# A factorization-machine kernel on one core: the raw quad moved to sixth place with a signal of its own, and VectorE scaling two quads of a block

## The reference

```python
gathered = jax.vmap(lambda table, idx: table[idx], in_axes=(0, 1), out_axes=1)(emb, xi)
e = gathered * xv[:, :, None]
s = jnp.sum(e, axis=1)
qi = 0.5 * (s * s - jnp.sum(e * e, axis=1))
h = jax.nn.relu(xv @ W1 + b1)              # hidden: 1024
x = jnp.concatenate([qi, h], axis=1)
return x @ W2 + b2                         # one number per sample
```

## Time and profile before

| | us |
|---|---|
| median of 3 runs (lowest to highest) | 735.56 (734.74 to 735.95) |
| the profiled execution | 734.71 |
| its span, first to last instruction | 732.9 |
| DVE busy | 540.5 |
| POOL busy | 485.9 |
| ACT busy | 474.2 |
| PE busy | 123.1 |

### The profile page before, as it was taken

How to read it: one execution, slowest core, us unless ns; L and a number is a source line. 1 busy time by engine, 2 the same in 40 slices (tenths; PEclk the granted TensorE clock), 3 DMA queues, 4 the chain that set the end, 5 groups by cost and what they waited for, 6 DMA issues and landing times.

```text
span 732.9 us, 2598 instructions
## 1 busy us (share of the span) xinstructions
PE 123.1 (17%) x374; PEld 29.6 (4%) x374; DVE 540.5 (74%) x463; ACT 474.2 (65%) x516; POOL 485.9 (66%) x524
## 2 busy tenths in 40 slices
PE   2030020300303003030211302203030220400315
PEld 0000000000000000000000000001000000000001
DVE  4675969595398683988969396396978849549684
ACT  0877775771875837778683863868777394567871
POOL 6777775762767737777774754777777474677760
PEclk9995555555555555555555555555555555555557
DMA  7777775772766737777774763777777474577760
GB/s 226 203 204 203 204 203 158 203 204 56 202 192 185 205 102 204 203 204 204 203 202 128 202 179 98 203 203 204 203 204 202 126 203 132 145 203 203 203 190 0
DMA packets 33683, 131.93 MB, mean 180 GB/s; under 512 B 8641, under 2 KB 8769, under 8 KB 33634
## 3 DMA queue, kind: packets, MB, share of 16 engines
q0 software_dynamic: 32768, 130.06, 64.6%
q1 hardware_dynamic: 800, 1.31, 0.6%
q10 hardware_dynamic: 98, 0.40, 0.2%
HBM read 131.72 MB, written 0.01 MB: 180 GB/s over the span
## 4 chain that ended last, share of the span: by engine, by line
POOL 39%; issue 23%; another core or an unknown queue 6%; PE 3%; DVE 2%; ACT 1%; DMA 0%; POOLq 0%
POOL gathered L218 39%; DVE running_ps L462 1%; PE sum_ps L328 1%; PE hidden_ps L349 1%; ACT squares L241 1%; ACT squares L247 1%; PE hidden_ps L362 1%; PE sum_ps L341 1%; DMA gathered<-emb,index_rows 0%; DVE squares L435 0%; DVE gathered L447 0%; POOLq L214 0%; DVE weighted_late L547 0%; DVE weighted L421 0%
## 5 line engine op out<-in xcount | busy, mean ns | idle before, releaser
L218 POOL DMA_INDIRECT gathered<-emb,index_rows x512 | 484.4, 946 | 224.1 <-issue 155.8
L462 DVE SCALAR_TENSOR_TENSOR running_ps<-gathered,running_ps 128x1984 f32<-128x1984 f32 x77 | 171.4, 2226 | 146.7 <-issue 107.6
L435 DVE SCALAR_TENSOR_TENSOR squares<-squares,w_ps 128x1984 f32<-128x1984 f32 (+1 forms) x128 | 276.7, 2167 | 0.0
L234 ACT ACTIVATE gathered<-gathered,values 128x496 f32<-128x496 f32 x312 | 194.5, 695 | 25.5 <-DMA gathered<-emb,index_rows 23.3
L241 ACT ACTIVATE squares<-gathered 128x5952 f32<-128x5952 f32 x31 | 159.8, 5156 | 36.8 <-DMA gathered<-emb,index_rows 34.3
L341 PE MATMUL sum_ps<-added_up,own_sample 128*32 128x496 f32 x128 | 30.1, 1031 | 550.3 <-issue 431.0
L247 ACT ACTIVATE squares<-gathered,values 128x496 f32<-128x496 f32 x76 | 47.4, 696 | 67.4 <-DMA gathered<-emb,index_rows 63.2
L362 PE MATMUL hidden_ps<-w_b,value_rows 33*128 33x512 f32 x64 | 55.3, 1011 | 42.4 <-issue 20.8
L234 ACT ACTIVATE running_ps<-gathered,values 128x496 f32<-128x496 f32 x64 | 39.5, 662 | 33.7 <-issue 18.7
L254 ACT ACTIVATE sum_squared<-sum_ps 128x496 f32<-128x496 f32 x16 | 9.2, 573 | 71.0 <-remote 58.4
L462 DVE SCALAR_TENSOR_TENSOR added_up<-gathered,running_ps 128x1984 f32<-128x1984 f32 x16 | 35.5, 2219 | 25.4 <-ACT gathered L234 25.0
(11 more groups left out here) (40 smaller groups left out, 27.0 us busy)
## 6 DMA issues: line engine op xcount, KB each, us to landing
gathered<-emb,index_rows POOLq DMA_INDIRECT x512
w_all<-w SPq DMA_DIRECT2D x1, 760.0 KB
values<-value SPq DMA_DIRECT2D x1, 256.0 KB, 2.9
value_rows<-value_t ACTq DMA_DIRECT2D x1, 256.0 KB
index_raw<-index SPq DMA_DIRECT2D x1, 240.0 KB, 4.3
w_b<-w ACTq DMA_DIRECT2D x1, 128.0 KB
index_raw<-index SPq DMA_DIRECT2D x1, 16.0 KB, 2.5
w_b<-b ACTq DMA_DIRECT2D x1, 4.0 KB
```

The costliest lines, as they stand in the source:

```text
L218: nc.gpsimd.indirect_dma_start(out=gathered[:, n % slots, j, :], out_offset=None, in_=emb, in_offset=bass.IndirectOffsetOnAxis(ap=index_ro ...
L234: return nc.scalar.mul(running_ps[:, j, 0:dim] if s == 0 else rows_of_one, rows_of_one, values[:, g:g + 1])
L435: return nc.vector.scalar_tensor_tensor(of, of, -0.5, w2_ps[:, 0:dim].unsqueeze(1).to_broadcast([P, quads_of.stop - quads_of.start, dim]), ...
L462: nc.vector.scalar_tensor_tensor(added_up[:, i % 2] if last_add(n) else sums, gathered[:, n % slots], 1.0, sums, ALU.mult, ALU.add).then_i ...
```

## The change

The raw quad of a block is no longer the eighth but the sixth (`block_quads = (5,)`), and `wide`, the quads that are added up, is now 0, 1, 2, 3, 4, 6 and 7, so that the last add of a block is that of quad 7. TensorE sums the raw quad before `added_up`, and its last matmul over the raw quad raises a new semaphore, `rows_summed`, for which POOL waits; `summed`, for which ACT and DVE wait, is raised by the last matmul over `added_up`. `by_vector` is now the quads 2 and 4, so DVE scales two quads of a block and ACT one fewer (1, 3, 6 and 7 beside quad 0). Their values don't fit into PSUM for 16 blocks: they are kept for eight at a time, by two copies at the start and two in block 7 at s = 6, when its quads 2 and 4 have been scaled (`keep_values`). ACT squares quads 4, 6 and 7 at the start of the next block, in two instructions, and the raw quad at s = 7. DVE weighs the hidden layer at s = 6 and the squared sums at s = 7.

```diff
-    block_quads = (7,)
-    wide = [0, 1, 2, 3, 4, 5, 6]
-    by_vector = 4
+    block_quads = (5,)
+    wide = [0, 1, 2, 3, 4, 6, 7]
+    by_vector = (2, 4)
+    kept_blocks = 8
...
-    square_of = {0: 1, 1: 2, 2: 2, 3: 2, 7: 3, 4: 4, 5: 4, 6: 4}
+    square_of = {0: 1, 1: 2, 2: 2, 3: 2, 5: 3, 4: 4, 6: 5, 7: 5}
...
                         if by_tensor(n - slots):
-                            pool.wait_ge(summed, (n - slots) // quads + 1)
+                            pool.wait_ge(rows_summed, (n - slots) // quads + 1)
...
-                if by_tensor(n):
-                    if s == (deep if i == end else quads - 1):
+                if i == end and s >= deep:
+                    if s == deep:
                         place_free(n)
                     square_quad(n)
-                elif s > 0 and s != by_vector:
+                elif s in by_scalar:
                     if s == 1:
                         begin_sums(n - 1)
                     scale_quad(n)
-                if s == 1:
+                if s == 0 and i > 0:
+                    square_scaled(n - 4, 1)
+                    square_scaled(n - 2, 2)
+                elif s == 1:
                     square_begun(n - 1)
...
                 elif s == 7:
-                    square_scaled(n - 3, 3)
+                    place_free(n)
+                    square_quad(n - 2)
...
                 if i > 0:
                     pe.wait_ge(sum_squared_ready, i)
-                pe.wait_ge(added, adds_with(i * quads + (3 if i == end else 6)))
-                sum_fields(i)
                 if i < end:
-                    sum_quad(i * quads + 7).then_inc(summed, 1)
+                    sum_quad(i * quads + block_quads[0]).then_inc(rows_summed, 1)
+                pe.wait_ge(added, adds_with(i * quads + (3 if i == end else 7)))
+                last = sum_fields(i)
+                if i < end:
+                    last.then_inc(summed, 1)
...
-                elif s == by_vector:
+                elif s in by_vector:
                     dve.wait_ge(fetched[n % slots], (n // slots + 1) * 16 * GROUPS)
                     nc.vector.scalar_tensor_tensor(
                         gathered[:, n % slots], gathered[:, n % slots], 1.0,
-                        running_ps[:, :, dim + i].unsqueeze(2).to_broadcast([P, GROUPS, dim]),
+                        running_ps[:, :, dim + 2 * (i % kept_blocks) + by_vector.index(s)].unsqueeze(2).to_broadcast([P, GROUPS, dim]),
                         ALU.mult, ALU.mult).then_inc(scaled_wide, 1)
...
+            def keep_values(first):
+                of = values[:].rearrange("p (i s j) -> p s j i", s=quads, j=GROUPS)
+                to = running_ps[:, :, dim:dim + 2 * kept_blocks].rearrange("p j (i t) -> p t j i", t=2)
+                for t in range(2):
+                    last = nc.vector.tensor_copy(to[:, t], of[:, by_vector[t], :, first:first + kept_blocks])
+                last.then_inc(values_kept, 1)
+                dve.wait_ge(values_kept, first // kept_blocks + 1)
+            keep_values(0)
...
+                if n % (quads * kept_blocks) == quads * kept_blocks - 2 and i < end:
+                    keep_values(i + 1)
...
-                if s == 6 and i > 0:
+                if s == 7 and i > 0:
                     weigh_sums(i - 1)
-                if s == 7 or n == end * quads + 4:
+                if s == 6 or n == end * quads + 4:
                     dve.wait_ge(hidden_ready, i + 1)
```

More of the change, by code:

```diff
@@ L47, in by_tensor, with scaled_wide_with @@
         return n % quads in (end_quads if n // quads == end else block_quads)
+    by_scalar = [s for s in wide[1:] if s not in by_vector]
     def scaled_with(n):
-        return n // quads * (adds - 1) + adds_with(n % quads) - (n % quads > by_vector)
+        i, s = divmod(n, quads)
+        return i * len(by_scalar) + max(sum(k <= s for k in by_scalar), 1)
+    def scaled_wide_with(n):
+        i, s = divmod(n, quads)
+        return i * len(by_vector) + sum(k <= s for k in by_vector)
     def adds_with(n):
@@ L58, in last_add @@
     def last_add(n):
-        return n % quads == (3 if n // quads == end else 6)
-    square_of = {0: 1, 1: 2, 2: 2, 3: 2, 7: 3, 4: 4, 5: 4, 6: 4}
+        return n % quads == (3 if n // quads == end else 7)
+    square_of = {0: 1, 1: 2, 2: 2, 3: 2, 5: 3, 4: 4, 6: 5, 7: 5}
     end_square_of = {0: 1, 1: 2, 2: 2, 3: 2, 4: 3, 5: 4, 6: 5}
@@ L68, in squared_with @@
         i, s = divmod(n, quads)
-        return i * 4 + (end_square_of if i == end else square_of)[s]
+        return i * 5 + (end_square_of if i == end else square_of)[s]
     lines = blocks * GROUPS
-    assert per * quads == fields and gathers == blocks * in_block and dim + blocks <= 512
+    assert per * quads == fields and gathers == blocks * in_block and dim + 2 * kept_blocks <= 512
     assert quads == 8
@@ L159, in fm_kernel @@
         normed = sem("normed")
+        rows_summed = sem("rows_summed")
         summed = sem("summed")
@@ L263, in square_scaled @@
                 act.wait_ge(scaled, scaled_with(n + count - 1))
-                if n % quads == by_vector:
-                    act.wait_ge(scaled_wide, n // quads + 1)
+                if any(n % quads <= s < n % quads + count for s in by_vector):
+                    act.wait_ge(scaled_wide, scaled_wide_with(n + count - 1))
                 square(n, count, slice(0, GROUPS)).then_inc(squared, 1)
@@ L328, in sum_rows @@
                 return nc.tensor.matmul(sum_ps[j * COLS:(j + 1) * COLS, 0:dim], operand,
-                                        gathered[:, n % slots, j], start=False,
-                                        stop=(s == quads - 1), tile_position=(0, j * COLS))
+                                        gathered[:, n % slots, j], start=(i < end),
+                                        stop=(n == all_quads - 1), tile_position=(0, j * COLS))
             def sum_quad(n):
@@ L341, in sum_fields @@
                     last = nc.tensor.matmul(sum_ps[j * COLS:(j + 1) * COLS, 0:dim], own_sample[:],
-                                            added_up[:, i % 2, j, :], start=True, stop=False,
+                                            added_up[:, i % 2, j, :], start=(i == end), stop=(i < end),
                                             tile_position=(0, j * COLS))
+                return last
             def late_squares(n):
@@ L448, in add_quad @@
                         gathered[:, n % slots], gathered[:, n % slots], 1.0,
-                        running_ps[:, :, dim + i].unsqueeze(2).to_broadcast([P, GROUPS, dim]),
+                        running_ps[:, :, dim + 2 * (i % kept_blocks) + by_vector.index(s)].unsqueeze(2).to_broadcast([P, GROUPS, dim]),
                         ALU.mult, ALU.mult).then_inc(scaled_wide, 1)
-                    dve.wait_ge(scaled_wide, i + 1)
+                    dve.wait_ge(scaled_wide, scaled_wide_with(n))
                 else:
@@ L481, in _ @@
             dve.wait_ge(values_loaded, 16)
-            nc.vector.tensor_copy(
-                running_ps[:, :, dim:dim + blocks],
-                values[:].rearrange("p (i s j) -> p s j i", s=quads, j=GROUPS)[:, by_vector]
-            ).then_inc(values_kept, 1)
+            def keep_values(first):
[6 more added lines that the diff above has]
+            keep_values(0)
             def spread(operands, of, count, unread):
@@ L496, in _ @@
                 spread(weights[:, :, j], values[:].rearrange("p (i s j) -> p i s j", s=quads, j=GROUPS
-                                                             )[:, :, quads - 1, j], blocks, j)
+                                                             )[:, :, block_quads[0], j], blocks, j)
             spread(end_weights[:].rearrange("p s j c -> p (s j) c"), values[:, gathers - deep * GROUPS:],
```

## The result

The changed kernel took 740.93 us (median of 4, 740.91 to 741.88) beside 735.15 us of the kernel before (median of 4): ratio 1.0088, 95% interval 1.0061 to 1.0115. It is 0.9% slower, where I had forecast 725.5 us, 1.4% faster; the time lies inside the range given, 692 to 750.

The account below looks back on a forecast made before the run. No engine was full; POOL's gather order, with 66.8 us of stops on late TensorE signals, was taken as the bound. 734.7 - 13 + 3 = 724.7 us, plus 0.85 for the median: 725.5 us, range 692 to 750.

Parts of the forecast that it names:

- the third term: POOL's standing still before gathers: 66.8 us, almost all in eight stops before a block's quad 7.
- The pace: TensorE's completions let go at one record per 2.80 us while gathers run: 56 us a block against 40 of gathers.
- The other signs: If right: 374 TensorE records, VectorE busy some 575 us, six or seven stops before quad 5, about 55 us in all.
- The cycle of four blocks: Kernel before: POOL's stops repeat every 178.9 us, 160 of gathers and 18.8 of stops.
- The slack: Time for TensorE's raw-quad signal before POOL asks: 15.5 us short before, 2.1 short after, so 13.4 us more.
- The -13 us: Gain over 16 blocks from fewer stops, 3.88 us a block in place of 4.70; bounds zero and 66.8.
- VectorE's second quad: VectorE scaling quad 2 as well: 16 more instructions, 35.5 us of work, forecast cost 0.
- the cover: VectorE's 6.06 us idle before a block's first add: scaling takes 2.2, leaving 3.8; without it, up to 35.5 us cost.
- The new order's 3 us: VectorE's weighing of the hidden layer, now before the last add, waits for late signals: 3 us, between 0 and 48.
- Moved squares and kept values: ACT's squares of quads 4, 6, 7 at the next block's start, and four copies keeping values: cost 0.
- The slower one: Rival: completions let go only when VectorE rests, so all eight stops grow 2.2 us: 753 us, chance 0.25.
- The rival that the stops move to quad 5 and stay: POOL's stops move from quad 7 to quad 5, their sum unchanged: 735.6 us, chance 0.13.

Follow-up runs that it names:

- e4: Kernel before without a raw quad in blocks 0 to 14, VectorE adding all eight quads: 736.81 us, ratio 0.9999.
- e5: The kernel of e4 with VectorE scaling quads 2 and 4 instead of 4 alone: 732.48 us, ratio 0.9971.
- e8: Changed kernel without the hidden layer's matmuls in blocks 1 to 15: 734.19 us (one run).
- e7: The kernel of e5 with small extra ScalarE instructions on six quads, 34 ScalarE instructions a block: 747.0 us (one run).
- e2: Changed kernel with VectorE scaling quad 4 alone, as before: 744.74 us, ratio 1.0109.
- e1: Kernel before with only VectorE's scaling of quads 2 and 4 added, raw quad still eighth: 742.43 us, ratio 1.0076.
- e17: The kernel of e2 again, on a chip where the kernel before takes 661.11 us: 661.57 us, ratio 1.0003.
- e12: Changed kernel with VectorE's weighing of the hidden layer put back behind the last add: 664.07 us, ratio 1.0038 (before: 661.74).
- e16: The kernel before itself, unchanged, run for its trace: 662.64 us.

## Why the prediction was wrong

*The first reading was right and its conclusion wrong.* The sum 4.3 + 640.4 + 66.8 + 21.4 + 1.8 holds, but "only the third term is open to a change of waits" does not. On the chips of the first kind the block takes about 44.8 us whatever POOL waits for: 44.73 before, 44.83 after, and 44.97 (e4), 44.80 (e5) and (607.14 - 427.71) / 4 = 44.86 (e8) in three kernels in which it never stops. By my estimate from these rows, 165 turns at 1.25 us and 346 at 1.40 put the start of the last gather at 4.3 + 206.3 + 484.4 = 695.0 at best, and 695.06 it was in e5; before, it starts at 710.21. At most 15 us of the 66.8 were to be had.

*The pace was read rightly.* One matmul record per 2.80 us, 56 us a block: between two late blocks of the changed kernel L264 moves by 498.11 - 442.11 = 56.00 us, for 20 records. Four records are 11.2 us apart again in two blocks (L264 at 660.51, L554 at 671.66); in three others it is 11.85. The other signs came too: 374 matmul records, 576 us of VectorE, six stops before quad 5. The mistake was to take the pace for TensorE's alone: ScalarE shows 1.40 us an instruction in e7, POOL in e5. The cycle of four blocks was read from blocks 8 to 13; blocks 2 to 5 had a stop each.

*The slack came, the step from slack to time failed.* "The stops come 13.4 / 16 = 0.84 block later: a cycle of 4.84 blocks in place of 4 for the same 18.8 us" is the step. They did come later, the first in block 4 in place of 2, and the cycle of four blocks became one of six. But its stops grew from 18.8 to 6 x 4.8 = 28.9 us. I had held the stops of a cycle fixed and let the cycle grow. In fact a stop pays off a debt, and the debt grows with each block: 4.7 us a block before, 4.8 after. More slack puts off the payment and changes nothing in the rate. The -13 us were -2.4, and those are, as I read it, a matter of where in the cycle the program ends.

*The end was left out.* I priced nothing behind the last gather. There the changed kernel takes 8.3 us more (e2: 9.8): its last stop ends at 694.11, many completions are still held back at the last gather, and the hidden sums are felt 40 us late, 21.5 before. Not all of it is the new order's: e1, in the old order, also has its last stop in block 15 and a tail 2.1 us longer than before. That leaves 6.2 us to the new order, in which twelve records and not four stand between POOL's signal and the hidden one. On chips with signals on time e17 shows 0.

*VectorE's second quad: 0 forecast, 5.6 measured alone (e1), 1.9 on the other chips.* On top of the moved raw quad no cost shows (e2 has 1.0109, the changed kernel 1.0088). In the middle the cover holds: in most blocks without a late signal VectorE still stands 3.3 to 3.9 us before its first add, 3.8 were forecast. At the end there is no cover, and in e1 the stops grow too. The new order's 3 us could not be told apart: in the middle L554 waited 3.8 to 4.5 us in five blocks, and what that cost is not shown; e12 makes it 0 where signals are on time. Moved squares and kept values: 0, as e17 shows for the squares.

*The rivals.* The slower one had the sign and not the mechanism: 753 from VectorE holding back the catching up. The rival that the stops move to quad 5 and stay, 735.6, was nearest to what the stops did; with 2.4 us less of stops and 8.3 more of tail it is the result. That the time lies inside my range is luck: its upper end, 750, was there for the slower rival, and its lower end is miscounted. The forecast gain is 10.1 us, and two and a half or three times that gives 710 or 705, not 692.

## What to carry to other kernels

When an engine waits for signals that come later than their work, count what the wait would be worth if it were gone by taking the waiting work out (e4), before moving it: a stop may be the place where a limit shows that lies elsewhere. If two kernels with different waits have the same time per block, look for what they issue the same number of. Price the end of the program by itself, and time a small effect on more than one chip.

## What the runs showed of the hardware

On the chips where the kernel before takes 735 us, signals were felt up to 40 us behind their matmuls, and while POOL issued gathers, and for 19 us behind the last one (e5), the spacing was 1.40 us an instruction on each engine that was late: 44.80 us for POOL's 32 gathers (e5), 47.60 for ScalarE's 34 instructions (e7), 2.80 for a matmul with its weight load. Then the engine itself was slowed. For POOL this rests on e5: in e4 ScalarE's 32 instructions and in e8 TensorE's 16 records would take 44.8 us as well. On the chips where it takes 662 us nothing of it is to be seen, with the same kernel and a like granted clock (0.599 in e16, 0.553 before). Between before and after the granted clock, 0.553 (at its half, the 1.2 GHz level, in most of the span) and 0.995, moved no time: L341 and L356, the same matmuls, take 1.03 us each way.

What the thing is stays open. The two groups of runs at 735 us ran on two chips, the three at 662 on three others and later, so that it may be the chip or something else that changed between them. Every timed execution was one that left records of its instructions. The Trainium skill's page "NOTIFIC — the notification-queue block", section "Overflow: three behaviours, one of which stalls the engine", says that such records can be set to hold up the engine that makes them. No run here shows that this is the cause. Nor was the kernel of gathers alone met by a chip of the first kind, so that POOL's 1.40 us were never seen without other engines at work beside it. And no kernel that gives the reference's result was shown to be faster than before by more than 0.3% (e5) on the first kind, or at all on the second.
